# A fused cross-attention and ternary FFN block: the start-up order of the first two batches, and the matmuls on a zero tile ahead of it

## What is computed

```
x1 = einsum('eth,efh->etf', n, c)            # scores, 120 per token
h  = gelu_tanh(x1) * x1
x  = x + einsum('etf,efh->eth', h, c)        # the weighted sum of context rows
n  = layernorm(x)
h  = silu(n @ w1.T * s1) * (n @ w2.T * s2)   # 256 -> 1024, "layer 1"
h  = gelu(h @ h1.T * s_h1); h = gelu(h @ h2.T * s_h2)   # 1024 -> 1024 each
x  = x + h @ w3.T * s3                       # 1024 -> 256
```

## Time and profile before

| | |
|---|---|
| median of 3 runs | 331.74 us |
| the profiled execution, its own time | 331.95 us |
| its span in the trace | 330.1 us |
| TensorE busy | 322.9 us (98%) |
| VectorE / ScalarE / GpSimd busy | 263.8 / 217.9 / 42.7 us |
| first matmul of layer 1 starts | 13.96 us |

### The profile page before, as it was taken

How to read it: one execution, slowest core, us unless ns; L and a number is a source line. 1 busy time by engine, 2 the same in 40 slices (tenths; PEclk the granted TensorE clock), 3 DMA queues, 4 the chain that set the end, 5 groups by cost and what they waited for, 6 DMA issues and landing times.

```text
span 330.1 us, 4723 instructions
## 1 busy us (share of the span) xinstructions
PE 322.9 (98%) x1627; PEld 272.8 (83%) x1627; DVE 263.8 (80%) x492; ACT 217.9 (66%) x367; POOL 42.7 (13%) x68
## 2 busy tenths in 40 slices
PE   7999999999999999999999999999999999999994
PEld 5799888888868888889998888888887888888994
DVE  4696996896995999998679566398899798987594
ACT  3556557655795886778834555977689687775840
POOL 4446011000000012103020002000000000110000
PEclk9999999999999999999999999999999999999998
DMA  7899999947747754745107033345575863453003
GB/s 235 277 332 221 207 273 382 362 159 278 238 168 259 245 199 127 199 157 171 49 2 254 3 127 127 130 127 191 201 237 192 286 233 127 127 139 117 0 32 105
DMA packets 23213, 60.22 MB, mean 182 GB/s; under 512 B 1680, under 2 KB 7568, under 8 KB 20624
## 3 DMA queue, kind: packets, MB, share of 16 engines
q0 software_dynamic: 13440, 37.75, 38.1%
q1 hardware_dynamic: 9744, 22.11, 20.0%
HBM read 49.36 MB, written 6.29 MB: 169 GB/s over the span
## 4 chain that ended last, share of the span: by engine, by line
PE 87%; DVE 6%; DMA 3%; issue 2%; ACT 1%; POOL 1%; SPq 0%; DVEq 0%; ACTq 0%
PE P L1306 53%; PE P L1258 18%; PE P L1335 9%; DMA SLY<-in_w 2%; PE P L1230 2%; PE P L1214 2%; PE P L1222 2%; DVE H L908 1%; DVE TR L913 1%; DVE H L929 1%; DMA xs<-in_x 1%; PE P L1407 1%; ACT TR L604 1%; PE P L1400 1%; POOL rs L432 1%
## 5 line engine op out<-in xcount | busy, mean ns | idle before, releaser
L1306 PE MATMUL P<-TR,WR 128*128 128x512 f32 x896 | 205.9, 390 | 0.3 <-DVE H L929 0.3
L1306 PEld LDWEIGHTS P<-TR,WR 128*128 128x128 f32 x896 | 167.5, 188 | 36.3 <-DVE H L929 1.1
L604 ACT ACTIVATE TR<-H 128x512 fp32r<-128x512 f32 x112 | 68.1, 626 | 30.0 <-DVE H L908 27.3
L913 DVE TENSOR_TENSOR TR<-H,TR 128x512 fp32r<-128x512 f32 x112 | 73.7, 685 | 8.3 <-ACT TR L604 6.6
L1258 PE MATMUL P<-X,W 128*128 128x512 f32 (+1 forms) x320 | 62.8, 352 | 0.1
L1258 PEld LDWEIGHTS P<-X,W 128*128 128x128 f32 x320 | 51.8, 189 | 8.0 <-DVE X L850 0.5
L908 DVE TENSOR_TENSOR H<-H 128x512 f32<-128x512 f32 x64 | 41.9, 682 | 0.0
L886 DVE SCALAR_TENSOR_TENSOR H<-P,sc,SLY 128x512 f32<-128x512 f32 (+1 forms) x40 | 25.2, 638 | 18.1 <-PE P L1258 10.2
L594 ACT ACTIVATE SLY<-P,sc 128x512 f32<-128x512 f32 (+1 forms) x40 | 23.7, 601 | 18.2 <-PE P L1258 14.7
L618 ACT ACTIVATE H<-P 128x512 f32<-128x512 f32 x48 | 27.7, 592 | 10.7 <-PE P L1306 10.7
L638 ACT ACTIVATE H<-H,sc 128x512 f32<-128x512 f32 x40 | 27.4, 713 | 10.7 <-DVE H L929 10.7
(11 more groups left out here) (73 smaller groups left out, 187.5 us busy)
## 6 DMA issues: line engine op xcount, KB each, us to landing
WR<-blocks_h POOLq DMA_DIRECT2D x16, 1024.0 KB, 5.0
WR<-in_h POOLq DMA_DIRECT2D x12, 1024.0 KB, 5.2
H<-in_h POOLq DMA_DIRECT2D x8, 512.0 KB, 12.0
blocks_h<-H SPq DMA_DIRECT2D x4, 1024.0 KB, 6.5
SLY<-in_h SPq DMA_DIRECT2D x8, 512.0 KB, 4.1
SLY<-in_w SPq DMA_DIRECT2D x6, 512.0 KB, 4.1
W<-in_w POOLq DMA_DIRECT2D x2, 1024.0 KB, 7.6
WR<-in_w POOLq DMA_DIRECT2D x2, 1024.0 KB, 5.9
```

The lines of the kernel that those rows point to most:

```text
L604: eng.activation(TR[:, f % RING, 0, :], operand(c, L, s, kk), ACT.Copy).then_inc(s_hi, 1)
L913: eng.tensor_tensor(TR[:, f % RING, 1, :], operand(c, L, s, kk), TR[:, f % RING, 0, :].bitcast(f32), ALU.subtract).then_inc(s_lo, 1)
L1306: out_ = eng.matmul(bank(c, L, s, m)[:, :], WR[r % WRING][:, at:at + 128], TR[:, f % RING, h, :], start=(s in FRESH[L] and kk == 0 and h = ...
```

## The change

- SyncE issues `x` of batch 1 ahead of batch 0's context tokens, and `x` of batch 2 ahead of the scale columns and of the wait for `load_w12(0)`.
- GpSimd no longer waits for ScalarE's table, and issues both loads of w1 and w2 behind the two `rstd_half(0, j)`. It computes one half of batch 1's `xn` (with a semaphore of its own, `e_xn`), VectorE the other, ahead of `gate_half(1)`. `rstd(1, 1)` comes ahead of the first load of h1.
- TensorE's first spins read a tile of zeros, `pad`, that VectorE fills as its first instruction. There are 18 of them, then single ones ahead of each `weigh_half`, and 2 ahead of `turn(0, 1)`, where there were 8.
- `score(1)` goes ahead of batch 0's second transposes, `weigh(1)` ahead of layer 1. ScalarE's `act_s(1)` and VectorE's `gate(1)` move up accordingly; `stats(1, 1)` comes ahead of all gate products, `stats(0, 2)` behind the first. `turn(1, 1)` and `turn(0, 2)` each come two groups sooner, and so do `first(1)` and `copy_t(2)` by one step of m.

```diff
-SPIN = (13, 8)
+SPIN = (18, 1, 1, 2)
...
+            load_x(1)
             eng.dma_start(ct[:, 0, 0, :], ctx_tok[:, 0, :]).then_inc(e_ct, 16)
-            load_x(1)
...
+            load_x(2)
             eng.dma_start(sc[:, :], cols).then_inc(s_sc, 16)
             eng.wait_ge(s_w12[0], 16)
-            load_x(2)
             load_x(3)
...
-            eng.wait_ge(s_tab, 1)
-            load_w12(0)
             rstd_half(0, 0)
             rstd_half(0, 1)
-            load_w12(1)
+            for i in range(2):
+                load_w12(i)
             rstd(0, 1)
             eng.wait_ge(s_rs[0], 2)
-            for j in range(2):
-                eng.tensor_scalar(xn[0][:, 1, j, :], ...).then_inc(s_xn[0], 1)
+            eng.tensor_scalar(xn[0][:, 1, 0, :], ...).then_inc(e_xn, 1)
             rstd_half(1, 0)
             rstd_half(1, 1)
+            rstd(1, 1)
+            load_w(0, 0, 0)
             rstd(0, 2)
-            load_w(0, 0, 0)
-            rstd(1, 1)
...  # ScalarE
-                    if m == 5:
+                    if m == 4:
                         first(1)
-                    if m == 7:
+                    if m == 6:
                         copy_t(2)
...
             copy_t(1)
+            act_s(1)
             first_half(0)
             first_half(1)
-            act_s(1)
             table(ACT.Silu)
...  # VectorE, in layer1(0)
                     if m == 0:
-                        stats(1, 1)
+                        stats(0, 2)
                     if m == 1:
+                        scale(1, 1)
+                    if m == 2:
                         scale(0, 2)
-                    if m == 2:
-                        scale(1, 1)
-                    if m == 5:
+                    if m == 4:
                         second(1)
...  # VectorE, at the start
+            eng.memset(pad[:, :], 0.0).then_inc(s_pad, 1)
...
             gate_half(0)
+            scale(0, 1)          # its j = 1 alone
             gate_half(1)
...
             scale_half(1, 1)
+            gate(1)
             second_half(0)
             second_half(1)
-            gate(1)
-            stats(0, 2)
             add_in(1)
+            stats(1, 1)
...  # TensorE, in layer1(0)
-                        if i == 2:
-                            weigh(1)
-                        if i == 11:
+                        if i == 9:
                             turn(1, 1)
-                        if i == 14:
+                        if i == 12:
                             turn(0, 2)
...  # TensorE, at the start
-            pad = ident[:, :].bitcast(bf16)
+            eng.wait_ge(s_pad, 1)
+            spin(SPIN[0])
             eng.wait_ge(s_id, 2)
-            spin(SPIN[0])
             turn_half(0, 0)
             turn_half(0, 1)
             score_half(0)
             score_half(1)
+            spin(SPIN[1])
             weigh_half(0)
+            spin(SPIN[2])
             weigh_half(1)
-            spin(SPIN[1])
+            spin(SPIN[3])
             turn(0, 1)
+            score(1)
             turn_half(1, 0)
             turn_half(1, 1)
-            score(1)
+            weigh(1)
```

More of the change, by code:

```diff
@@ L71, in xattn_ffn @@
         spare = sb("spare", [128, 2], f32)
+        pad = sb("pad", [128, 256], bf16)
         early = ExitStack()
@@ L130, in xattn_ffn @@
         s_chk = [sem(f"s_chk{i}") for i in range(4)]
-        s_id, s_one, s_mh, s_eps = sem("s_id"), sem("s_one"), sem("s_mh"), sem("s_eps")
+        s_id, s_one, s_mh, s_eps, s_pad = sem("s_id"), sem("s_one"), sem("s_mh"), sem("s_eps"), sem("s_pad")
         s_st = [sem("s_st1"), sem("s_st2")]
@@ L138, in xattn_ffn @@
         s_s, s_o = sem("s_s"), sem("s_o")
-        e_mv, e_rs, e_tr, e_xt, e_s = (sem(f"e_{n}") for n in ("mv", "rs", "tr", "xt", "s"))
+        e_mv, e_rs, e_xn, e_tr, e_xt, e_s = (sem(f"e_{n}") for n in ("mv", "rs", "xn", "tr", "xt", "s"))
         e_gl, e_h, e_o, e_x2, e_X0 = (sem(f"e_{n}") for n in ("gl", "h", "o", "x2", "X0"))
@@ L146, in xattn_ffn @@
         s_m4, s_y, s_y2, s_out = sem("s_m4"), sem("s_y"), sem("s_y2"), sem("s_out")
-        s_tab, s_ab, s_fl, s_fp, s_ft = sem("s_tab"), sem("s_ab"), sem("s_fl"), sem("s_fp"), sem("s_ft")
+        s_ab, s_fl, s_fp, s_ft = sem("s_ab"), sem("s_fl"), sem("s_fp"), sem("s_ft")
         g_w, g_in, g_out = sem("g_w"), sem("g_in"), sem("g_out")
@@ L470, in load_sum @@
                 eng.dma_start(place(r), wS[("h1", "h2")[L]][STORED[s]].rearrange("p k o -> p (k o)")).then_inc(s_w[r % WRING], 16)
-            eng.wait_ge(s_tab, 1)
-            load_w12(0)
             rstd_half(0, 0)
             rstd_half(0, 1)
-            load_w12(1)
+            for i in range(2):
+                load_w12(i)
             rstd(0, 1)
             eng.wait_ge(s_rs[0], 2)
-            for j in range(2):
-                eng.tensor_scalar(xn[0][:, 1, j, :], xs[:, 2 + j, :], mv[:, 0, 1, j, 0:1], rs[:, 0, 1, j:j + 1],
-                                  ALU.subtract, ALU.mult).then_inc(s_xn[0], 1)
+            eng.tensor_scalar(xn[0][:, 1, 0, :], xs[:, 2, :], mv[:, 0, 1, 0, 0:1], rs[:, 0, 1, 0:1],
+                              ALU.subtract, ALU.mult).then_inc(e_xn, 1)
             rstd_half(1, 0)
             rstd_half(1, 1)
+            rstd(1, 1)
+            load_w(0, 0, 0)
             rstd(0, 2)
-            load_w(0, 0, 0)
-            rstd(1, 1)
             load_w(0, 0, 5)
@@ L546, in table @@
             def table(func):
-                eng.activation(spare[:, :], mhalf[:, :], func).then_inc(s_tab, 1)
+                eng.activation(spare[:, :], mhalf[:, :], func)
             def copy_t(b):
@@ L802, in scale @@
             def scale(norm, b):
-                if (norm, b) == (0, 2):
-                    eng.wait_ge(s_tr[0], 2)
-                elif b >= 2:
+                if b >= 2:
                     eng.wait_ge(s_tr[norm], b - 1)
@@ L809, in scale @@
                 eng.wait_ge(s_rs[norm], b + 1)
-                for j in range(2):
+                for j in range(1 if (norm, b) == (0, 1) else 0, 2):
                     eng.tensor_scalar(xn[norm][:, b % 2, j, :], xs[:, 2 * b + j, :], mv[:, norm, b % 4, j, 0:1],
@@ L1211, in turn @@
                 for j in range(2):
-                    eng.wait_ge(s_xn[norm], 2 * b + j + 1)
+                    if (norm, b, j) == (0, 1, 0):
+                        eng.wait_ge(e_xn, 1)
+                    else:
+                        eng.wait_ge(s_xn[norm], 2 * b + j + (0 if norm == 0 and b >= 1 else 1))
                     for c in range(2):
```

## The result

The changed kernel takes 330.17 us, the median of 7 runs (329.87 to 330.47), beside 331.82 us for the kernel before (7 runs, 331.25 to 332.79). The medians lie 1.65 us apart, a quotient of 0.9950; the ratio that goes with the 95% interval of 0.9919 to 0.996 is 0.9939. So the kernel is faster by its interval, by 0.5 to 0.6%. The forecast was 330.4 us, in a range of 329.6 to 332.2. The bound for "faster" stood at 330.08: the median is 0.09 us above it, on the side of "no change" that had the chance of 0.72, while the ratio would put it on the other side.

What follows compares the result with a forecast made beforehand. TensorE, full from layer 1's start at 13.96 us, was taken as the bound. From the profiled 331.95 us, 0.87 for weigh(1) and 0.69 for layer 1's earlier start came off: 330.39, or 330.4 us, range 329.6 to 332.2.

Steps and rivals of the forecast that it cites:

- What bounds the kernel: TensorE is busy nearly throughout from 14 to 326 us; work ahead counts only through layer 1's start at 13.96 us.
- if a stretch behind 40 us changes its length: Sign that the prediction is wrong; the rest of the span was to keep its length less 0.87 us.
- The first spins: TensorE's start: 18 spins from about 1.0 us end at 4.85, before the first transpose at 4.97; cost 0 to 0.1 us, taken as 0.
- weigh(1) out of layer 1: Batch 1's weighted sum leaves TensorE's full stretch: gain 0.87 to 1.1 us, taken as 0.87; the first groups' 0.26 us may partly go.
- Where turn(0, 1) starts and the chain from it: Ahead of layer 1: turn(0, 1) at 9.0 us plus batch 1's chain of 4.27 starts layer 1 at 13.27, 0.69 sooner.
- The early rise as the likeliest case: TensorE reaches 2.4 GHz at about 5 us, near the end of the first spins: 330.4 us, chance 0.46.
- as late as before: Rival: TensorE's clock rises at 10.66 us, layer 1 starts at 14.97, 1.0 later: 332.1 us, chance 0.15.
- The slower side: Rival: no clock rise by 13 us, layer 1 starts at the lower level at 17.4, 3.4 later: 334.5 us, chance 0.05.
- GpSimd and VectorE: Rival: computing batch 1's xn halves, they shut each other out, delaying gate_half(1) by 1.22 us: 331.6 us, chance 0.05.
- w1 and w2 later: Loads issued at about 5.0 and 5.7 us land at 11.9 to 13.3 and 12.6 to 14.0, in time: cost 0.
- the term for the DMA work behind the start: SyncE's batch 3 x and contexts of batches 2 and 3 wait for w1 and w2 landings; readers over 8 us behind: nothing.
- the forecast of no measurable change: Whole kernel: time between 330.08 and 333.40 us, about 0.5% (1.66 us) either way, chance 0.72; faster 0.22, slower 0.06.

Runs made afterwards that it cites:

- w1 load first: The changed kernel with the first load of w1 and w2 issued ahead of both rstds of batch 0, the second behind them: 336.41 us, ratio 1.0141 to before.
- h1 early: The changed kernel with both loads of h1's first blocks issued ahead of rstd(1, 1): 329.76 us, ratio 0.9955 to the kernel before.

## Why the prediction was right

*What bounds the kernel* held: from layer 1's start on, each stage is TensorE's own length, equal to 0.06 us in all profiles of the same order within layer 1, except for w1 load first, the one late block sum and the stage from the products to w3 (87.2 to 88.0 us). By the prediction's own sign, "if a stretch behind 40 us changes its length", it was wrong there: two of them did, by 0.44 and 0.20 us. What the change did is in the first 32 us.

*The first spins* cost nothing, as taken: they end at 4.75 us (or 5.06), the first transpose starts at 5.08, 0.1 us later than before, the 0 to 0.1 of the forecast. It waited 0.32 us for xn there, so the spins did not hold it.

*weigh(1) out of layer 1*, 0.87 us: 0.83 between the profiles, 0.85 by experiment. The further 0.26 us of the first groups was not got back.

*Where turn(0, 1) starts and the chain from it*: forecast 9.0 + 4.27 = 13.27, measured 8.85 + 4.24 = 13.09 in one profile, 9.19 + 4.25 = 13.44 in the other. The 4.27 is well founded. The 9.0 came by a path that did not hold: I had `weigh_half(1)` wait until 8.33 for VectorE's scale of batch 1 and the gate behind it. That gate ended at 7.97 us, `weigh_half(1)` started at 8.12 straight behind its spin, and the chain that ended last runs through the gate and the weighted sum of batch 0's first half (L836 at 7.07, L1414 at 7.50). The two paths were level to within 0.1 us, so the sum came out, with some luck. Batch 0's second norm was expected to be ready before, and was: X ended at 12.86 us. With `weigh(1)` taken away it let layer 1 start at 13.01, so the two paths are almost level, and the last link of batch 1's chain costs 0.08 to 0.17 us.

*The early rise as the likeliest case* held in every profile with 18 spins: the half scores took 1.1 to 1.3 us, not 2.03, in all ten, the one of the spins put alone on the kernel before among them. The case "as late as before" was right in its mechanism and its front (14.97 forecast, 14.88 measured with 13 spins); its total of 332.1 was too high by 1 us, for the most part since it was built on the profiled execution of before, whose stage from 65 to 153 us was 0.8 us longer than in that run (88.01 against 87.19). The Trainium skill ("TensorE: Matmul & The Clock Gate", Part 1) says that the moment of the rise is run-variable. The traces agree: 10.66 us and about 6 in the two profiles of the kernel before, 4.2 and later than 4.9 in the two of the changed one. This also means that the 331.95 from which I subtracted was an execution with a late rise; the kernel before has early ones too, and against the 331.24 us of its second profile the changed kernel's two are 0.8 and 1.3 us ahead, not 1.5.

*The slower side* did not come with a late rise: with no spins at all, layer 1 started at 15.07 us and at 2.4 GHz. It came with a late x, in w1 load first, and there its sum was near (6.38 us for the chain where I had 6.7).

*GpSimd and VectorE* did not shut each other out. In three profiles VectorE's scale beside GpSimd's took 0.41, 0.53 and 0.63 us, and GpSimd's took 1.35, 1.23 and 1.23. The rows of one of them:

```profile
7.58 0.53 DVE L808 TENSOR_SCALAR xn<-xs,mv,rs 128x256 f32<-128x256 f32 x1
```

```profile
7.42 1.23 POOL L481 TENSOR_SCALAR xn<-xs,mv,rs 128x256 f32<-128x256 f32 x1
```

The Trainium skill ("SBUF — State Buffer", "Who interferes with whom") says that the later of the two fully blocks if VectorE's operation is in one of its two-port modes. The traces show no such block, which would have cost some 1.2 us: GpSimd's took 0.13 us at most over the 1.22 of the earlier trace rows, and VectorE's 0.22 at most over the shortest, 0.41. Which mode VectorE's scale was in, no run shows. The row that I had set against this rival was weak: VectorE's two of 4.50 to 5.57 ran beside GpSimd's rstd and the issue of a load, not beside a scale of GpSimd's.

*w1 and w2 later, at no cost*: nothing was lost at layer 1's start, but the loads took 7.9 and 9.7 us to land where I had taken 6.9 to 8.3, so the first was there at 12.8 us, 0.3 ahead of layer 1. That the block sum was late at 63.7 us was not foreseen: the term for the DMA work behind the start stood at nothing. The late loads cut the room ahead of the products, as h1 early and w1 first show from the other side (8.7 and 10.1 us instead of 6.25 and 7.1), each in one profile; why this cost 0.44 us in one execution and nothing in the next stays open.

*Two errors that cancelled.* Between the first two profiles the front gave 0.18 us more than forecast, and the stages behind it took 0.24 back. And the forecast of no measurable change, 0.72, is right by 0.09 us only, the distance of the median from the bound of 330.08. The sum's 1.56 us was itself only 0.1 us short of the 1.66, which deserved more than 0.22 for "faster".

## What to carry to other kernels

When one engine is busy from some point to the end, split a change into what happens ahead of that point (measured by the start of the first full-stretch instruction) and what is taken out behind it; here the two gave 0.87 and 0.83 us, and each was forecast to 0.2 us. A clock that rises early is worth only what the next chain lets through: 0.41 us in the kernel before, where TensorE then waited for GpSimd's xn, and 1.4 to 1.8 us in the changed one. An instruction set ahead in an in-order queue carries its own inputs' lateness to all behind it: one load issued 0.4 us ahead of a small one cost some 6 us. And one profile of the kernel before is not enough to put a gain down to an edit: here its two differ by 0.41 us at layer 1's start.

## What the runs showed of the hardware

- The granted clock of a window reads 1.00 at the start of every profile, though the matmuls there are 213 ns apart for 256 columns (1.2 GHz). Up to 30 us it read 0.50 only in the run with w1 load first, after TensorE had stood idle for 3.79 us. So in these profiles the level at the start can be read only from the distance of the starts.
- The moment of the rise moves between executions of one kernel: about 6 us and 10.66 us in the two profiles of the kernel before. With no spins at all it came at 10.5 to 10.8 us, after TensorE had worked from 5.21 us on.
- A 1 MB load issued 0.4 us ahead of a 256 KB one from another queue delayed the landing of the small one from under 5.4 to 9.8 us; issued 0.7 us behind it, no delay shows. Issued 0.26 us behind it (2.84 and 2.58 us), the small one was there at 6.1 us in two profiles and by 5.63 in a third.
- The kernel before against itself gave a ratio of 1.0078, interval 1.0054 to 1.0102, from four executions on one side.
